# AdaLN + routed-LoRA feed-forward, one core: constant operand for the filling products, and picking products that stream the whole table

## What is computed

```python
W = weights[condition]                                 # (64, 32, 32) out of (16, 32, 32)
y = einsum('bct,bcd->bdt', x, W)                       # x: (64, 32, 512)
result = einsum('bnd,od->bno', y, W_base) + b_base     # 512 x 512
probs = softmax(einsum('bnd,ed->bne', y, W_gate))      # 8 experts
route_w = the two largest of probs, divided by their sum, at their experts, else 0
h = einsum('bnd,erd->bner', y, A)                      # 8 experts x 16 ranks
delta = einsum('bner,eor->bno', h * route_w[..., None], B)
out = x + result + delta
```

## Time and profile before

| what | us |
|---|---|
| median of three runs | 97.15 |
| the three runs | 96.89, 97.15, 97.41 |
| the profiled execution, its own time | 96.82 |
| its span, first to last instruction | 95.0 |
| PE busy | 90.9 |
| DVE busy | 65.6 |
| ACT busy | 23.6 |
| POOL busy | 16.2 |

### The profile page before, as it was taken

The page is one execution under the profiler, slowest core; times in us unless marked ns, Lnnn a source line. Parts: engine busy times, 40 slices in busy tenths (PEclk is TensorE's granted clock), DMA queues, the critical chain, the costliest instruction groups (busy, mean ns, idle before and its releaser), DMA issues.

```text
span 95.0 us, 1835 instructions
## 1 busy us (share of the span) xinstructions
PE 90.9 (96%) x651; PEld 88.6 (93%) x651; DVE 65.6 (69%) x234; ACT 23.6 (25%) x56; POOL 16.2 (17%) x29
## 2 busy tenths in 40 slices
PE   4999999999999999999999999999999999999980
PEld 1499999999999999999999999999999999999970
DVE  3686977867675866867675767767676758668880
ACT  5147613311304031311313040312213040311300
POOL 5167303030303030120303030210300000000000
PEclk9999999999999999999999999999999999999999
DMA  2999171240607051331607060332507020302005
GB/s 37 293 342 359 63 240 57 91 138 26 209 0 219 9 185 49 128 100 50 178 0 218 17 212 16 116 116 87 146 10 216 0 110 0 110 7 110 0 16 205
DMA packets 6360, 10.65 MB, mean 112 GB/s; under 512 B 1008, under 2 KB 1616, under 8 KB 6352
## 3 DMA queue, kind: packets, MB, share of 16 engines
q1 hardware_dynamic: 5760, 10.25, 32.8%
q0 software_dynamic: 448, 0.23, 1.0%
q10 hardware_dynamic: 144, 0.07, 0.2%
HBM read 6.35 MB, written 4.19 MB: 111 GB/s over the span
## 4 chain that ended last, share of the span: by engine, by line
PE 95%; DVE 1%; issue 0%; DVEq 0%
PE main_ps L492 56%; PE y_ps L474 15%; PE main_ps L512 12%; PE main_ps L580 3%; PE hwT_ps L462 3%; PE hwT_ps L502 2%; PE main_ps L528 2%; PE y_ps L574 1%; PE hwT_ps L474 1%; DVE x_sb L455 0%; DVEq L67 0%; DVE warm L310 0%; PE main_ps L522 0%; DVEq L454 0%
## 5 line engine op out<-in xcount | busy, mean ns | idle before, releaser
L492 PE MATMUL main_ps<-w_lo,y_hi 128*128 128x320 f32 x120 | 28.8, 321 | 0.0
L492 PE MATMUL main_ps<-w_hi,y_hi 128*128 128x320 f32 x120 | 28.8, 320 | 0.0
L492 PE MATMUL main_ps<-w_hi,y_lo 128*128 128x320 f32 x120 | 27.6, 311 | 0.0
L241 POOL DMA_INDIRECT mixw<-cond_w,row_ids x14 | 14.0, 998 | 48.9 <-PE y_ps L474 47.0
L492 PEld LDWEIGHTS main_ps<-w_hi,y_lo 128*128 128x128 f32 x120 | 20.3, 188 | 0.0
L492 PEld LDWEIGHTS main_ps<-w_lo,y_hi 128*128 128x128 f32 x120 | 19.8, 189 | 0.1
L492 PEld LDWEIGHTS main_ps<-w_hi,y_hi 128*128 128x128 f32 x120 | 19.4, 190 | 0.0
L474 PE MATMUL y_ps<-mix,x_sb 128*128 128x128 f32 x124 | 17.3, 284 | 0.0
L474 PEld LDWEIGHTS y_ps<-mix,x_sb 128*128 128x128 f32 x124 | 16.5, 200 | 0.0
L274 ACT ACTIVATE second<-top 128x1 f32<-128x1 f32 x16 | 4.7, 296 | 44.6 <-DVE top L375 44.6
L415 DVE TENSOR_TENSOR x_sb<-main_ps,x_sb 128x512 f32<-128x512 f32 x15 | 10.4, 691 | 5.4 <-PE main_ps L512 5.3
(11 more groups left out here) (66 smaller groups left out, 75.4 us busy)
## 6 DMA issues: line engine op xcount, KB each, us to landing
x_sb<-x SPq DMA_DIRECT2D x16, 256.0 KB, 2.9
out<-x_sb SPq DMA_DIRECT2D x15, 256.0 KB
w_raw<-w_all SPq DMA_DIRECT2D x4, 324.0 KB, 3.3
b_raw<-b_lora SPq DMA_DIRECT2D x1, 256.0 KB
bias_sb<-bias SPq DMA_DIRECT2D x1, 256.0 KB, 3.7
out<-x_sb SPq DMA_DIRECT2D x2, 128.0 KB
mixw<-cond_w,row_ids POOLq DMA_INDIRECT x14, 2.5
table<-cond_w ACTq DMA_DIRECT2D x1, 64.0 KB, 2.1
```

The costliest lines, as they stand in the source:

```text
L241: pool.indirect_dma_start(mixw[:, t, :], None, cond_w, bass.IndirectOffsetOnAxis(row_ids[:, t:t + 1], 0))\
L492: last = pe.matmul(main_ps[t % 2][:, half, 0:n_cols], y, w[:, half * HALF:half * HALF + n_cols], start=i == 0, stop=i == STEPS - 1)
```

## The change

The filling products take their operand from a tensor of ones that the framework writes ahead of the kernel's own instructions: one column of bf16, read with a step of 0 as 128 or 512 columns. Both memsets, both semaphores and both waits of TensorE go. The conditions' product takes its ones from there too. Five filling products of 512 columns stand ahead of it in place of three of 512 and one of 256; the two behind it stay. Each picking product has all four blocks of the split table as its moving operand, 256 columns instead of 64, and writes 256 columns of PSUM, shifted by the block, so that the 64 wanted ones of each block fall on the same place `PICKED_AT`; what falls beside it is read by nobody.

```diff
-    WARM_BEFORE, WARM_BEHIND = (512, 512, 512, 256), (512, 512)
+    WARM_BEFORE, WARM_BEHIND = (512,) * 5, (512, 512)
...
-        warm = sb("warm", [P, 512], bf16)
-        ones = sb("ones", [P, P], bf16)
+        ones = nc.const_aps.tensor(1.0, [P, 512], bf16)
...
-        picked_ps = [main_ps[t][:, 0, 0:2 * C].rearrange("p (s d) -> p s d", s=2) for t in range(PICKED)]
+        PICKED_AT = (K - 1) * 2 * C
+        picked_ps = [main_ps[t][:, 0, PICKED_AT:PICKED_AT + 2 * C].rearrange("p (s d) -> p s d", s=2)
+                     for t in range(PICKED)]
...
-            dve.memset(warm[:, :], 0.0).then_inc(warm_ready, 1)
-            dve.memset(ones[:, :], 1.0).then_inc(ones_ready, 1)
...
-                    pe.matmul(hwT_ps[1][:, 0:n], warm[:, 0:P], warm[:, 0:n], start=True, stop=True)
+                    pe.matmul(hwT_ps[1][:, 0:n], ones[:, 0:P], ones[:, 0:n], start=True, stop=True)
...
-            pe.wait_ge(warm_ready, 1)
             warm_up(WARM_BEFORE)
-            pe.wait_ge(ones_ready, 1)
             pe.wait_ge(own_cond_ready, 1)
-            pe.matmul(cond_ps, ones[:, :], own_cond[:, :, :], start=True, stop=True).then_inc(cond_spread, 1)
+            pe.matmul(cond_ps, ones[:, 0:P], own_cond[:, :, :], start=True, stop=True).then_inc(cond_spread, 1)
             warm_up(WARM_BEHIND)
             pe.wait_ge(table_lo_ready, 1)
             for t in range(PICKED):
                 for k in range(K):
                     pe.wait_ge(pick_ready, t * K + k + 1)
-                    last = pe.matmul(picked_ps[t], pick[:, t, k, :, :], table_split[:, k, :, :],
-                                     start=k == 0, stop=k == K - 1)
+                    shifted = main_ps[t][:, 0, PICKED_AT - k * 2 * C:PICKED_AT + (K - k) * 2 * C]
+                    last = pe.matmul(shifted, pick[:, t, k, :, :], table_split[:, :, :, :],
+                                     start=k == 0, stop=k == K - 1, skip_group_check=True)
                 last.then_inc(picked, 1)
```

More of the change, by code:

```diff
@@ L133, in adaln_ffn_kernel @@
         bias_landed = sem("bias_landed")
-        warm_ready = sem("warm_ready")
         first_channel_ready = sem("first_channel_ready")
@@ L149, in adaln_ffn_kernel @@
         first_mixw_ready = sem("first_mixw_ready")
-        ones_ready = sem("ones_ready")
         rows_ready = sem("rows_ready")
```

## The result

The changed kernel takes 95.97 us at the median of six runs (95.83 to 96.31), the kernel before 97.28 beside it (six runs, 96.86 to 97.74). The ratio is 0.9855, interval 0.9816 to 0.9894. The changed kernel was measured again in two later sessions, with ratios of 0.9807 (0.9729 to 0.9885) and 0.9864 (0.9821 to 0.9906).

The account below looks back on a forecast made before the run. TensorE's dense products bound the kernel, so gains in the first 12 us move the end. Profiled 96.82 less 0.64 gives 96.18; the median's 0.33 above gives 96.51, and recovering a third of 0.33 gives 96.4; range 96.0 to 97.3.

Parts of the forecast that it names:

- What bounds the kernel: Whole kernel: TensorE is busy 90.9 of 95.0 us, so what the first 12 us gain moves the end equally.
- The rise moves well ahead of 8.1: TensorE's clock, front: with the break filled and picks streaming throughout, it rises between 3.80 and 8.1 us, well before 8.1.
- Memsets out, fill from 0.80: Start of the kernel: without waiting for DVE's memset, TensorE's filling products begin at 0.80 us, 0.39 earlier.
- Five of 512 end at 2.93: Filling products ahead of the conditions' product: five end at 2.93 to 2.97 us; up to 0.25 of delay costs nothing.
- Whole-table picks cost nothing in throughput and 0.16 in latency: Picking products: 256 columns fit the existing 0.213 us spacing at the low clock; a tile's last pick ends 0.16 later.
- One sign that I had named: Chain by time, the eight picking products: they would take 1.71 us or less together.
- The moment counts little, because ACT's third split ends the gain at 0.64 to 0.72: L492, chunk 2: waiting for ACT's split leaves 0.64 us of 1.14; any clock rise up to about 6.3 gives this.
- The sum: Whole kernel: 96.82 less 0.64 is 96.18; the median's 0.33 above gives 96.51; a third of 0.33 recovered gives 96.4.
- its second term: Spread of the runs: if later clock rises cause part of it, the change recovers a third of 0.33 us.
- (A): Rival, chance 0.24: the clock's rise doesn't move enough, staying at 8.1 (97.2 us) or coming at 7.7 (97.05).
- (B): Rival, chance 0.13: the clock's rise varies by run and the change moves only its odds; median 96.8 us.
- (C): Rival, chance 0.07: the filling operand with step 0 along its columns streams at half rate; slower, 98.1 us.

Follow-up runs that it names:

- before_again: The kernel before, with no edit, measured again to see how its runs differ: ten runs, 96.8 to 98.1 us, the profiled one 97.93.

## Why the prediction was right or wrong

**What bounds the kernel**: right. In the first profile of the change everything behind 13 us moved as one block, by 0.50.

**The rise moves well ahead of 8.1**: right in its direction, and wrong in its grounds. I took the first pick (3.80) as the earliest moment, and the record has 3.41 in one run. I gave the break and the thin picks as the two causes together, with the early start as a third. The picks alone do it in eleven runs of eleven. The fill, with the start at 0.78 and no break, does it in seven of ten, the filled break alone in two of four, by their times. The change needs only its third part; with the third there, no run shows a gain from the first two beyond the spread.

**Memsets out, fill from 0.80**: 0.78. **Five of 512 end at 2.93**: the conditions' product starts at 2.87 instead of 2.98, and the delay that I had allowed for wasn't needed.

**Whole-table picks cost nothing in throughput and 0.16 in latency**: the eight loads take 1.78 as before, and the latency is 0.13 to 0.16. With the stream four times as long the picks keep their spacing, so it was the load that had set it at 64 columns. The Trainium skill ("TensorE: Matmul & The Clock Gate", "LDWEIGHTS (loading the stationary operand)") gives 107 ns for such a load; by that the picks would have cost 0.85 us more than before, and the traces show no such loss. One sign that I had named didn't come: the eight picks take 1.84 in the chain, not 1.71 or less, because the last one's stream ends later, and nothing is lost by it.

**The moment counts little, because ACT's third split ends the gain at 0.64 to 0.72**: this step failed. The mechanism exists: PE waits for `w_hi` at chunks 1 and 2 in the first profile of the change (0.12 and 0.24) and, more, in the second (0.6), and both keep 0.50 of span with rises 2.75 us apart. But I took the landing times of one execution as fixed, and wrote "0.64 to 0.72, whichever lands last". In the last profile the splits end at 9.55 instead of 10.15, nothing waits, and the gain is 1.21, about the 1.14 that I had worked out before I cut it. The profile of before_again shows the same of the kernel before: its splits, held by no transfer, end at 9.91. Against its profiled run of 96.82 the change's median of 95.97 is 0.85 less, where the sum had 0.64. The terms of the sum were thus 0.64 + 0.11 = 0.75 and came out as 0.85 + 0.46 = 1.31.

**The sum**: its second term was missized most, at 0.11 where 0.46 came. I saw that the median lay 0.33 above the profiled run and that a later rise in other runs might be why, and took a third of it. The rise is at 8.1 in one of the fastest executions of the kernel before (96.82) and at 10.6 in a slow one (97.93), a difference of 1.11 us of time. The change takes all of that away: its slowest of sixteen runs is 96.31. So of the 1.3 us of gain, 0.5 is what the two first profiles show, another 0.46 is the median of before above its first profile (97.28 against 96.82), and 0.34 is the first profile of the change above its median (96.31 against 95.97).

**Rivals.** (A) fell: the three profiles of the change have the rise at 3.41, about 4.0 and 6.16, and by the times no run has it at 8.1. (B), the rise as a matter of the run, is true of the kernel before and, by their times, of the kernels with only the earlier fill or only the filled break. As B put it, with some executions of the change gaining all and others little, it fell: all its runs are early, though at different moments. The Trainium skill ("TensorE: Matmul & The Clock Gate", "What's actually happening") says that the observation is free-running, so that the transition shifts by 500 ns either way between runs. The shift is there, since TensorE's products in two traces of one kernel agree within 0.02 us until 7.59 and the clock then rises 2.5 us apart; its size here is larger than the page gives. (C) fell: the operand with step 0 streams like any other, five products in 2.29 us by ends, and the weights load from it in 0.10 to 0.15, as they did from the stored one (0.10 to 0.15).

## What to carry to other kernels

Where a front at the low clock stands ahead of a dense stream of products, look at how many columns each product there streams beside how long its weights load: picks of 64 columns look as busy as picks of 256 (PE busy for 1.70 of 1.70 us from 3.8 to 5.5 in both first profiles). Columns up to the load's own spacing (0.213 here) cost latency alone, and here they brought more than the filling products did. And if the fastest and slowest runs of a kernel lie over 1% apart, don't take one profile's moments, of the clock's rise or of a landing, as fixed: ask what the change does to each kind of run.

## What I had not expected

The clock's rise in one and the same kernel came at 8.1 and at 10.6 us, with all of TensorE's products until 7.59 equal within 0.02 us. A kernel without any filling product (96.19 to 97.20) beats one with six and thin picks (96.72 to 98.31), by 1.2 us at the medians of one session. A memset of bf16 ones takes 0.48 us, of bf16 zeros 0.27, for the same 512 columns.
